# Criss-cross attention: the attention matmuls stream 96 instead of 128 columns of the turned weights

## The chip, the cores and the metric

The kernel runs on one core of a Trainium2 chip. The metric is the device time of one execution in microseconds (us). The core has TensorE (PE in the profile, with its weight loads as PEld), VectorE (DVE), ScalarE (ACT), GpSimd (POOL), SyncE (SP, which here issues all DMAs) and 16 DMA engines. SBUF is the working memory; TensorE writes into eight PSUM banks of 128 partitions x 512 fp32 values.

## The reference, cut to what matters

The input x is 8 x 512 x 96 x 96 (batch, channels, rows, columns), fp32. Every position attends to the positions of its own column and its own row:

```python
q = einsum('oc,bchw->bohw', Wq, x) + bq        # 64 channels
k = einsum('oc,bchw->bohw', Wk, x) + bk        # 64 channels
v = einsum('oc,bchw->bohw', Wv, x) + bv        # 512 channels
energy_H = einsum('bchw,bcgw->bhwg', q, k) - 1e30 * eye(96)[None, :, None, :]
energy_W = einsum('bchw,bchv->bhwv', q, k)
att = softmax(concatenate([energy_H, energy_W], -1), -1)
att_H, att_W = att[..., :96], att[..., 96:]
out_H = einsum('bcgw,bhwg->bchw', v, att_H)
out_W = einsum('bchv,bhwv->bchw', v, att_W)
return gamma * (out_H + out_W) + x
```

The change is about the last two products. For one column w (or one row h) each is a matrix product of 512 channels x 96 positions with 96 positions x 96 positions.

## The kernel before, in words

Each of the 8 batches passes through the same stages, and X (all of x for one batch, 128 partitions x 4 channel tiles x 9216 positions) stays in SBUF.

1. **Projection.** 24 chunks of 384 positions. ScalarE and GpSimd split x into two fp32r parts; TensorE makes k and q (`project_kq`, L724) and v (`project_v`, L708), and the energies along rows (`row_energies`, L734). v, k, q and the exponentials go to DRAM.
2. **Column energies.** 24 groups of four columns: TensorE multiplies k and q (L745), VectorE takes maxima and sums, ScalarE the exponentials, GpSimd masks the diagonal.
3. **Attention.** 24 chunks of four columns (the column half), then 24 chunks of four rows (the row half). For a chunk, SP loads the exponentials Pe (L220) and the values V (L224). GpSimd scales Pe by the softmax factors (L388), TensorE turns it with four transposes (`turn`, L755), ScalarE copies the result from PSUM to Pt (L474), and TensorE multiplies V with it (`attend`, L766): per column or row one product for each of four channel tiles of 128. VectorE adds the four products of one column or row, 384 values per partition, to X (`add_attention`, L608). In the row half the finished parts of X are stored, and the next batch's x comes in. The batch that is last stores through its whole row half; the others store little there and do the rest in the next projection.

V, Pe, Pt and the turned PSUM tiles have three buffers, so chunk g+1 is turned before chunk g is multiplied, and SP asks for V of a chunk when the multiplication three chunks before it has ended. The PSUM output of `attend` rotates over four banks, one per column or row of the chunk. The order on each engine is the order of the program; nothing is planned at run time.

The reference's 96 positions are the contraction rows: V and Pt hold zeros in partitions 96 to 127, so a 128-row product can be used (`attend` names `V[:, ...]` and `Pt[:, ...]` over all partitions). Along the free axis the moving operand is `Pt[:, c, r * N:r * N + WIDE]` with WIDE = 128: the 96 columns of this row and 32 more, which are those of the next row or, after the last row of a chunk, 32 zeros that GpSimd writes at L413. Their results are never read: VectorE takes `[:, :, 0:N]` of each group of 128. An fp32 matmul appears in the trace as two LDWEIGHTS and two MATMULs, so the 6144 products of L766 are 12288 of each; a transpose is one of each.

Of the kernel before, what the change touches and what calls it, by code (L numbers as in the profile page):

```python
# [12 lines left out]
N = 96  # L13
POS = N * N
ROWS = 4
CP = ROWS * N
# [9 lines left out]
RING = 3  # L26
TRIPLES = CHUNKS // RING
HALVES = 2
WIDE = 128


def criss_cross_attention(nc, x, wqk_t, wv_t, bqk, bv, gamma, out):
    B, C = x.shape[0], x.shape[1]
    CT = C // P
# [15 lines left out]
    with ctx:  # L50
        def sb(name, shape, dt=F32, at=None):
            return (at or ctx).enter_context(nc.sbuf_tensor(name, shape, dt))

        def sem(name):
            return ctx.enter_context(nc.semaphore(name))
# [29 lines left out]
        with ExitStack() as s3:  # L85
            V = sb("V", [P, RING, ROWS, C], F32, s3)
            ident = sb("ident", [N, N], F32, s3)
            Pe = sb("Pe", [N, RING, ROWS, N], F32, s3)
            Pt = sb("Pt", [P, RING, CP + WIDE - N], F32, s3)
            st = sb("st", [N, 4, N], F32, s3)  # L90
# [7 lines left out]
        t_ps, f_ps, o_ps = bank[2:5], bank[5], bank[6:8] + bank[0:2]  # L98
# [47 lines left out]
        pt_padded = sem("pt_padded")  # L146
# [8 lines left out]
        def g_no(b, along, p, c):  # L155

            return b * (2 * CHUNKS) + CHUNKS * along + p * RING + c
# [10 lines left out]
        def past(s, n):  # L168

            return n + START[s]  # L170
# [195 lines left out]
        @block.gpsimd  # L366
        def _(pool):
            def split_x(b, p, c):

                for h, cts in enumerate(halves):  # L370
                    pool.wait_ge(x_hi_made, (b * CHUNKS + p * 2 + c) * HALVES + h + 1)
                    nc.gpsimd.tensor_tensor(x_split[:, c % 2, 1, cts, :], X[:, cts, bass.ds((p * 2 + c) * CP, CP)],  # L372
                                            x_split[:, c % 2, 0, cts, :].bitcast(F32), ALU.subtract)\
                        .then_inc(x_lo_made, 1)

            def mask(b, p, c):

                pool.wait_ge(c_exped, b * GROUPS + p * RING + c + 1)
                pool.sem_inc(pool_passed, 1)
                nc.gpsimd.affine_select(out=E_cols[:, c, :, :], in_=E_cols[:, c, :, :], compare_op=ALU.not_equal,  # L380
                                        fill=0.0, base=0, pattern=[[0, GROUP], [-1, N]], channel_multiplier=1)\
                    .then_inc(c_masked, 1)

            def scale(b, along, p, c):
                pool.wait_ge(p_in[c], 16 * (b * (2 * TRIPLES) + along * TRIPLES + p + 1))

                f = mx[:, along, bass.ds((p * RING + c) * ROWS, ROWS)].unsqueeze(2).to_broadcast((N, ROWS, N))
                nc.gpsimd.tensor_tensor(Pe[:, c, :, :], Pe[:, c, :, :], f, ALU.mult)\  # L388
                    .then_inc(p_scaled, 1)

            def make_ident(times_before):
                nc.gpsimd.memset(ident[:, :], 0.0).then_inc(ident_made, 1)
                pool.wait_ge(ident_made, times_before * 2 + 1)
                pool.sem_inc(pool_passed, 1)
                nc.gpsimd.affine_select(out=ident[:, :], in_=ident[:, :], compare_op=ALU.not_equal, fill=1.0,
                                        base=0, pattern=[[-1, N]], channel_multiplier=1).then_inc(ident_made, 1)

            make_ident(0)
            with pool.Fori(0, B) as b:
                with pool.Fori(0, PAIRS) as p:  # L400
                    for c in range(2):
                        split_x(b, p, c)
                with pool.Fori(0, TRIPLES - 1) as p:
                    for c in range(RING):
                        mask(b, p, c)
                mask(b, TRIPLES - 1, 0)

                pool.wait_ge(c_summed, past(c_summed, (b + 1) * (2 * GROUPS)))
                pool.sem_inc(pool_passed, 1)
                make_ident(b + 1)  # L410
                mask(b, TRIPLES - 1, 1)
                mask(b, TRIPLES - 1, 2)
                nc.gpsimd.memset(Pt[0:N, :, CP:], 0.0).then_inc(pt_padded, 1)  # L413
                nc.gpsimd.memset(Pt[N:P, :, :], 0.0).then_inc(pt_padded, 1)
                nc.gpsimd.memset(V[N:P, 0, :, :], 0.0).then_inc(v_padded[0], 1)
                for along in range(2):

                    pool.wait_ge(f_made, b * 2 + along + 1)
                    pool.sem_inc(pool_passed, 1)
                    with pool.Fori(0, TRIPLES) as p:  # L420
                        for c in range(RING):
                            scale(b, along, p, c)
# [111 lines left out]
        def _(dve):  # L534
# [64 lines left out]
            def add_attention(b, along, p, c):  # L599
                for r in range(ROWS):  # L600
                    n = g_no(b, along, p, c) * ROWS + r
                    dve.wait_ge(o_summed, past(o_summed, n + 1))
                    at = (p * RING + c) * ROWS + r
                    if along:
                        xs = X[:, :, bass.ds(at * N, N)]
                    else:
                        xs = X[:, :, :].rearrange("p t (h w) -> p t h w", w=N)[:, :, :, at]
                    nc.vector.tensor_tensor(xs, o_ps[r][:, :].rearrange("p (t n) -> p t n", t=CT)[:, :, 0:N], xs,  # L608
                                            ALU.add).then_inc(o_added, 1)

            with dve.Fori(0, B) as b:
# [81 lines left out]
        def _(pe):  # L693
# [64 lines left out]
            def attend(b, along, p, c):  # L758
# [3 lines left out]
                for r in range(ROWS):  # L762

                    pe.wait_ge(o_added, past(o_added, g * ROWS + r - 3))
                    for ct in range(CT):
                        last = nc.tensor.matmul(o_ps[r][:, ct * WIDE:(ct + 1) * WIDE],  # L766
                                                V[:, c, r, ct * P:(ct + 1) * P], Pt[:, c, r * N:r * N + WIDE],
                                                start=True, stop=True)
                    last.then_inc(o_summed, 1)

            with pe.Fori(0, B) as b:
                def step(p, c, first=False):
                    project_kq(b, p, c)
                    if first:
                        pe.wait_ge(w_lo_made, 2)

                        pe.wait_ge(o_added, past(o_added, b * (2 * CHUNKS * ROWS)))
                    project_v(b, p, c, 0)
                    project_v(b, p, c, 1)
                    row_energies(b, p, 2 * c)  # L780
                    project_v(b, p, c, 2)
                    row_energies(b, p, 2 * c + 1)

                for c in range(2):
                    step(0, c, first=(c == 0))
                with pe.Fori(1, PAIRS) as p:
                    for c in range(2):
                        step(p, c)


                pe.wait_ge(ident_made, (b + 1) * 2)
                pe.wait_ge(z_summed, b * (SUBS + GROUPS) + SUBS)
                nc.tensor.transpose(t_ps[0][0:N, 0:N], mx[:, 1, :], ident[:, :])
                nc.tensor.transpose(t_ps[0][0:N, N:2 * N], zs[:, 1, :], ident[:, :]).then_inc(st_turned, 1)

                pe.wait_ge(e_shifted, past(e_shifted, (b + 1) * SUBS))
                for c in range(RING):
                    column_energies(b, 0, c)
                with pe.Fori(1, TRIPLES) as p:
                    for c in range(RING):  # L800
                        column_energies(b, p, c)


                pe.wait_ge(ident_made, (b + 2) * 2)
                pe.wait_ge(f_turned, b * 2 + 1)
                nc.tensor.transpose(f_ps[0:N, 0:N], st[:, 0, :], ident[:, :]).then_inc(f_turned, 1)

                pe.wait_ge(pt_padded, (b + 1) * 2)  # L810
                for j in range(RING):
                    pe.wait_ge(v_padded[j], b + 1)
                turn(b, 0, 0, 0)
                for along in range(2):
                    with pe.Fori(0, TRIPLES - 1) as p:
                        for c in range(RING):
                            turn(b, along, p + (c + 1) // RING, (c + 1) % RING)
                            attend(b, along, p, c)
                    for c in range(RING):
                        if c < RING - 1:  # L820
                            turn(b, along, TRIPLES - 1, c + 1)
                        elif along == 0:
                            turn(b, 1, 0, 0)
                        attend(b, along, TRIPLES - 1, c)
# [23 lines left out]
```

## Time and profile before

| | |
|---|---|
| time, three runs | 4355.52, 4362.07 (median), 4365.45 us |
| span of the profiled execution, first to last instruction | 4357.4 us |
| PE busy | 4063.6 us, 93% |
| PEld busy | 3654.3 us, 84% |
| DVE / ACT / POOL busy | 50% / 30% / 26% |
| mean granted TensorE clock | 0.936 of full speed |
| HBM traffic | 947.78 MB, 217 GB/s over the span |

The profile gives the span of its execution and no time beside it; the span lies within the three runs' times, 4.7 us below their median. The busy share of PE counts a matmul until its result has drained, so it is not the share of the time in which the array takes in columns; for that one reads the distance between the starts of successive instructions. The granted clock is given per stretch: 1.00 is the level of 2.4 GHz, 0.50 that of 1.2 GHz. A batch takes about 540 us: some 270 us of projection, 60 us of column energies with what lies around them, and 200 us of attention.

### The profile page before, as it was taken

What the parts mean: (1) busy time and instruction counts of PE and PEld (TensorE: products, weight loads), DVE (VectorE), ACT (ScalarE), POOL (GpSimd) and SP (SyncE); (2) the same over time, 40 slices, a digit from 0 to 9 for tenths busy, and PEclk for the clock granted to TensorE, in tenths of its full rate; (3) what the DMA queues carried; (4) which work ended last, traced back from release to release, by engine and by line L of the source; (5) the groups of instructions that cost most, each with busy time, mean ns of one, the idle gap of its engine ahead of it and who ended that gap; (6) DMA issues with size and microseconds to landing.
All of it is one profiled execution on the core that took longest, in us unless ns stands there. A gap on an engine that the chain in (4) does not pass through costs nothing.

```text
span 4357.4 us, 92393 instructions
## 1 busy us (share of the span) xinstructions
PE 4063.6 (93%) x26136; PEld 3654.3 (84%) x26136; DVE 2184.9 (50%) x3932; ACT 1288.8 (30%) x2522; POOL 1148.6 (26%) x1006
## 2 busy tenths in 40 slices
PE   8989999898998999989999899997999979999897
PEld 7878988788887998879988699886988869988697
DVE  3348533485334853348433484335843358433584
ACT  3342133421334213341133411335113351133510
POOL 3322133221332213322233222332223322233211
PEclk9988999889998999979999799997999979999799
DMA  5548977489774897749977499774997749977499
GB/s 177 172 150 213 247 231 244 153 219 253 232 238 146 222 256 229 247 136 229 249 236 239 136 232 245 246 238 134 234 239 243 240 137 232 252 237 232 148 243 315
DMA packets 555124, 947.78 MB, mean 218 GB/s; under 512 B 45120, under 2 KB 383552, under 8 KB 533568
## 3 DMA queue, kind: packets, MB, share of 16 engines
q1 hardware_dynamic: 555072, 947.30, 75.2%
q14 instruction: 46, 0.38, 0.0%
q8 instruction: 6, 0.10, 0.0%
HBM read 550.77 MB, written 396.36 MB: 217 GB/s over the span
## 4 chain that ended last, share of the span: by engine, by line
PE 82%; DMA 9%; issue 3%; ACT 2%; SPq 1%; POOL 1%; DVE 0%; ACTq 0%; POOLq 0%; DVEq 0%
PE bank L708 36%; PE bank L766 26%; PE bank L724 9%; DMA Pe<-e_scratch 7%; PE bank L745 5%; PE bank L734 3%; PE bank L755 3%; ACT kq L461 1%; DMA KQ<-kq_scratch 1%; POOL Pe L388 1%; ACT E L466 1%; DMA kq_scratch<-kq 1%; POOL x_split L372 0%; SPq L224 0%; DVE X L608 0%
## 5 line engine op out<-in xcount | busy, mean ns | idle before, releaser
L708 PE MATMUL bank<-Wv_hi,x_split 128*128 128x512 f32 x4608 | 1525.6, 399 | 0.0
L766 PE MATMUL bank<-Pt,V 128*128 128x128 f32 x12288 | 1478.4, 280 | 0.0
L766 PEld LDWEIGHTS bank<-Pt,V 128*128 128x128 f32 x12288 | 1436.7, 196 | 0.0
L608 DVE TENSOR_TENSOR X<-bank,X 128x384 f32 (+1 forms) x1536 | 1115.4, 734 | 559.1 <-PE bank L766 559.0
L372 POOL TENSOR_TENSOR x_split<-X,x_split 128x768 fp32r<-128x768 f32 x384 | 702.3, 1854 | 1411.1 <-ACT x_split L435 1411.0
L555 DVE TENSOR_TENSOR v_out<-bank,bv_row 128x512 f32<-128x512 f32 x576 | 398.3, 691 | 1287.3 <-PE bank L708 1281.2
L708 PEld LDWEIGHTS bank<-Wv_hi,x_split 128*128 128x128 f32 x4608 | 867.9, 188 | 189.0 <-issue 0.5
L708 PE MATMUL bank<-Wv_lo,x_split 128*128 128x512 f32 x2304 | 912.5, 396 | 0.0
L388 POOL TENSOR_TENSOR Pe<-Pe,mx 96x384 f32<-96x384 f32 x384 | 316.6, 824 | 1288.6 <-DMA Pe<-e_scratch 1287.8
L474 ACT ACTIVATE Pt<-bank 96x384 f32<-96x384 f32 x384 | 187.3, 488 | 1424.9 <-PE bank L755 1424.9
L446 ACT ACTIVATE kq<-bank,bqk_sb 64x192 f32<-64x192 f32 x768 | 320.6, 417 | 812.1 <-PE bank L734 645.8
L708 PEld LDWEIGHTS bank<-Wv_lo,x_split 128*128 128x128 f32 x2304 | 434.3, 188 | 88.1
L745 PE MATMUL bank<-KQ,kq 128*96 (+1 forms) x1536 | 329.2, 370 | 106.4 <-ACT kq L461 91.9
L724 PE MATMUL bank<-x_split,Wqk_hi 128*128 128x384 f32 x1536 | 409.7, 348 | 16.0 <-POOL x_split L372 16.0
L745 PEld LDWEIGHTS bank<-KQ,kq 128*96 128x96 f32 x1536 | 266.4, 253 | 169.1 <-issue 164.5
L452 ACT ACTIVATE E<-E 96x192 f32<-96x192 f32 x384 | 139.7, 364 | 605.2 <-DVE E L568 585.1
L435 ACT ACTIVATE x_split<-X 128x768 fp32r (+1 forms) x384 | 303.7, 838 | 47.5 <-PE bank L766 39.1
L755 PE MATMUL bank<-ident,Pe 96*96 96x96 f32 x1536 | 201.6, 255 | 100.7 <-POOL Pe L388 100.1
L724 PEld LDWEIGHTS bank<-x_split,Wqk_hi 128*128 128x128 f32 x1536 | 266.9, 190 | 18.5 <-issue 12.1
L724 PE MATMUL bank<-x_split,Wqk_lo 128*128 128x384 f32 x768 | 259.4, 338 | 0.0
L755 PEld LDWEIGHTS bank<-ident,Pe 96*96 96x96 f32 x1536 | 152.2, 130 | 119.8 <-POOL Pe L388 106.3
L461 ACT ACTIVATE kq<-KQ 64x192 f32 (+1 forms) x384 | 202.7, 530 | 139.8 <-DMA KQ<-kq_scratch 89.2
(45 smaller groups left out, 1551.9 us busy)
## 6 DMA issues: line engine op xcount, KB each, us to landing
V<-v_scratch SPq DMA_DIRECT2D x384, 768.0 KB, 5.7
X<-in_x SPq DMA_DIRECT2D x192, 768.0 KB, 5.1
v_scratch<-v_out SPq DMA_DIRECT2D x576, 256.0 KB, 3.8
out<-X SPq DMA_DIRECT2D x192, 768.0 KB, 6.3
Pe<-e_scratch SPq DMA_DIRECT2D x384, 144.0 KB, 5.3
kq_scratch<-kq SPq DMA_DIRECT2D x384, 96.0 KB, 2.3
e_scratch<-E SPq DMA_DIRECT2D x384, 72.0 KB, 1.7
e_scratch<-E SPq DMA_DIRECT2D x192, 144.0 KB, 1.9
```

Source lines behind the costliest of these rows:

```text
L372: nc.gpsimd.tensor_tensor(x_split[:, c % 2, 1, cts, :], X[:, cts, bass.ds((p * 2 + c) * CP, CP)], x_split[:, c % 2, 0, cts, :].bitcast(F32 ...
L388: nc.gpsimd.tensor_tensor(Pe[:, c, :, :], Pe[:, c, :, :], f, ALU.mult)\
L435: nc.scalar.activation(x_split[:, j, 0, cts, :], X[:, cts, bass.ds((p * 2 + c) * CP, CP)], ACT.Copy).then_inc(x_hi_made, 1)
L446: last = nc.scalar.activation(kq[0:CQ, i, :], kq_ps[c % 2][rows, v * SP_:(v + 1) * SP_], ACT.Identity, bias=bqk_sb[rows, :])
L461: nc.scalar.activation(kq[0:CQ, v, :].rearrange("p (w h) -> p w h", w=2), src, ACT.Copy)\
L555: nc.vector.tensor_tensor(v_out[:, s, :], v_ps[t % 2][:, :], bv_row[:, :], ALU.add)\
L608: nc.vector.tensor_tensor(xs, o_ps[r][:, :].rearrange("p (t n) -> p t n", t=CT)[:, :, 0:N], xs, ALU.add).then_inc(o_added, 1)
L708: last = nc.tensor.matmul(v_ps[t % 2][:, :], x_split[:, j, lo, ct, at], w[:, ct, :], start=(ct == 0 and n == 0), stop=(ct == CT - 1 and n ...
L724: last = nc.tensor.matmul(kq_ps[j][:, 0:CP], w[:, ct, :], x_split[:, j, lo, ct, :], start=(ct == 0 and n == 0), stop=(ct == CT - 1 and n = ...
L745: last = nc.tensor.matmul(ce_ps[c][0:N, at:at + N], kq[:, v, r * N:(r + 1) * N], k, start=True, stop=True)
L755: last = nc.tensor.transpose(t_ps[c][0:N, r * N:(r + 1) * N], Pe[:, c, r, :], ident[:, :])
L766: last = nc.tensor.matmul(o_ps[r][:, ct * WIDE:(ct + 1) * WIDE], V[:, c, r, ct * P:(ct + 1) * P], Pt[:, c, r * N:r * N + WIDE], start=True ...
```

## The change

WIDE becomes 96. Each matmul of L766 then streams the 96 columns of its own row, its four outputs lie next to each other in the first 384 columns of the bank, Pt shrinks from 416 to 384 columns per buffer, and the memset of its last 32 columns goes, with one step of the semaphore `pt_padded`. The zero partitions 96 to 127 stay. No instruction moves to another place in any engine's order; GpSimd has one memset less per batch and a narrower one (L414: 1152 columns for 1248).

```diff
-WIDE = 128
+WIDE = 96
@@ GpSimd, before the attention stage of each batch
-                nc.gpsimd.memset(Pt[0:N, :, CP:], 0.0).then_inc(pt_padded, 1)
                 nc.gpsimd.memset(Pt[N:P, :, :], 0.0).then_inc(pt_padded, 1)
@@ add_attention
-                    nc.vector.tensor_tensor(xs, o_ps[r][:, :].rearrange("p (t n) -> p t n", t=CT)[:, :, 0:N], xs,
+                    nc.vector.tensor_tensor(xs, o_ps[r][:, 0:CT * WIDE].rearrange("p (t n) -> p t n", t=CT)[:, :, 0:N], xs,
                                             ALU.add).then_inc(o_added, 1)
@@ TensorE, before the first turn of each batch
-                pe.wait_ge(pt_padded, (b + 1) * 2)
+                pe.wait_ge(pt_padded, b + 1)
```

The matmul itself reads WIDE and is written as before:

```python
last = nc.tensor.matmul(o_ps[r][:, ct * WIDE:(ct + 1) * WIDE],
                        V[:, c, r, ct * P:(ct + 1) * P], Pt[:, c, r * N:r * N + WIDE],
                        start=True, stop=True)
```

## Rows read from the trace of the kernel before

**Rows 1.** Page, part 4: the chain that ended last, by engine and line.
```profile
PE 82%; DMA 9%; issue 3%; ACT 2%; SPq 1%; POOL 1%; DVE 0%; ACTq 0%; POOLq 0%; DVEq 0%
PE bank L708 36%; PE bank L766 26%; PE bank L724 9%; DMA Pe<-e_scratch 7%; PE bank L745 5%; PE bank L734 3%; PE bank L755 3%; ACT kq L461 1%; DMA KQ<-kq_scratch 1%; POOL Pe L388 1%; ACT E L466 1%; DMA kq_scratch<-kq 1%; POOL x_split L372 0%; SPq L224 0%; DVE X L608 0%
```

**Rows 2.** Page, part 5: busy us, mean ns of one, idle before.
```profile
L766 PE MATMUL bank<-Pt,V 128*128 128x128 f32 x12288 | 1478.4, 280 | 0.0
L766 PEld LDWEIGHTS bank<-Pt,V 128*128 128x128 f32 x12288 | 1436.7, 196 | 0.0
```

**Rows 3.** Busy time by stretch; last three columns clock, DMA share, GB/s.
```profile
305.00:338.00 33.00, 31.30 (x145) 25.34 (x145) 26.93 (x55) 28.38 (x54) 9.47 (x18) 0.50 0.28 80
350.00:355.00 5.00, 5.00 (x26) 5.00 (x25) 1.65 (x2) 0.49 (x1) 0.82 (x1) 0.50 0.97 252
356.00:440.00 84.00, 84.00 (x772) 84.00 (x772) 76.55 (x86) 10.56 (x22) 17.32 (x21) 1.00 0.93 233
446.00:500.00 54.00, 53.67 (x486) 52.88 (x486) 31.15 (x55) 6.45 (x14) 11.52 (x14) 1.00 1.00 235
500.00:549.00 49.00, 40.95 (x341) 39.84 (x340) 20.63 (x38) 4.75 (x10) 7.41 (x9) 0.94 1.04 274
4250.00:4340.00 90.00, 69.69 (x607) 66.47 (x607) 37.91 (x68) 8.02 (x17) 13.99 (x17) 1.00 1.06 326
```

**Rows 4.** Chain of waits inside the column half: start us, us, piece.
```profile
928.89 0.33 PE bank L755 x4
929.23 3.60 PE bank L766 x32
932.83 0.33 PE bank L755 x4
```

**Rows 5.** Single weight loads in order of time, full clock: start us, us.
```profile
356.39 0.13 PEld L755 LDWEIGHTS bank<-ident,Pe 96*96 96x96 f32 x1
356.50 0.13 PEld L755 LDWEIGHTS bank<-ident,Pe 96*96 96x96 f32 x1
...
356.75 0.19 PEld L766 LDWEIGHTS bank<-Pt,V 128*128 128x128 f32 x1
356.86 0.19 PEld L766 LDWEIGHTS bank<-Pt,V 128*128 128x128 f32 x1
356.97 0.19 PEld L766 LDWEIGHTS bank<-Pt,V 128*128 128x128 f32 x1
```

**Rows 6.** The same at half clock, first loads of an attention stage.
```profile
350.25 0.34 PEld L766 LDWEIGHTS bank<-Pt,V 128*128 128x128 f32 x1
350.47 0.33 PEld L766 LDWEIGHTS bank<-Pt,V 128*128 128x128 f32 x1
350.68 0.33 PEld L766 LDWEIGHTS bank<-Pt,V 128*128 128x128 f32 x1
```

**Rows 7.** Chain of waits, projection stage: the row energies.
```profile
1103.56 0.34 PE bank L734 x4
```

**Rows 8.** TensorE in order of time: a stage start, and a fall of the clock.
```profile
350.41 6.25 PE L766 MATMUL bank<-Pt,V 128*128 128x128 f32 x32
...
4237.42 3.76 PE L766 MATMUL bank<-Pt,V 128*128 128x128 f32 x32
4243.66 0.88 PE L755 MATMUL bank<-ident,Pe 96*96 96x96 f32 x4 [2.48 <-POOL Pe L388]
4244.33 4.95 PE L766 MATMUL bank<-Pt,V 128*128 128x128 f32 x32
```

**Rows 9.** VectorE in order of time, column half.
```profile
902.79 3.57 DVE L608 TENSOR_TENSOR X<-bank,X 128x384 f32 x4 [0.37 <-PE bank L766]
```

**Rows 10.** Instructions on tile Pt: ns min/median/max, first and last start.
```profile
L413 POOL MEMSET Pt<- x8: 176/180/181, 343.5 to 4126.3; 96x96 f32 x8
```

**Rows 11.** Chain of waits at the start of an attention stage.
```profile
885.38 5.41 DMA Pe<-e_scratch
```

## The prediction

> **What bounds the kernel now.** I read the page's chain first: TensorE is 82% of it, L766 alone 26% and L755 3%, and the loads of Pe are 7% [rows 1]. So the changed matmuls lie on the path, with some 26% of 4357.4, about 1130 us. The second view is the busy time by stretch, because the attention stage is not one thing. In the column half TensorE never pauses (84.00 of 84.00 us) and the DMA engines are at 0.93. In the row half TensorE still hardly pauses, but the DMA share is 1.00; at its end, and through the row half of the batch that is last, it is 1.04 to 1.06 and TensorE waits [rows 3]. Third, the chain inside the column half: 0.33 us for four transposes and 3.60 us for 32 matmuls, nothing else, so a chunk takes 3.93 us [rows 4]. A pair of weight load and matmul therefore takes 3.60 / 32 = 112.5 ns. The question is which of the two sets it. The totals do not tell: both are busy for nearly the same time [rows 2]. Last I read single loads one after another, and the granted clock.
>
> **Is it the load or the streaming?** For the streaming: the row energies, 96 columns moving against 96-column weights, take 0.34 / 4 = 85 ns each [rows 7], and the L766 pairs with 128 against 128 take 112.5. Both numbers fit two passes of the moving columns at 2.4 GHz (80 and 107 ns) plus about 5, and both fit a load of the same width. The case that separates them is a wide load behind a narrow matmul, which occurs once per chunk. The first 128-column load of L766 starts at 356.75, while the last 96-column transposes are still streaming (a transpose takes 0.33 / 4 = 83 ns [rows 4]). If streaming set the pace, the next load would start 0.08 us later. It starts 0.11 later, at 356.86, and the one after it again 0.11 later [rows 5]. At half clock the same place shows 350.25 to 350.47, 0.22 us, then 0.21 [rows 6]; a 96-column matmul takes about 0.16 there. So loading 128 columns of V takes as long as streaming the 128 padded columns twice, at either clock level, and the load is not touched by the change. The matmul becomes shorter than the load that hides behind it, and the pair stays where it is.
>
> By the Trainium skill ("TensorE: Matmul & The Clock Gate", "LDWEIGHTS") a load takes its columns divided by 1.2 GHz, 107 ns for 128. The 0.11 us agree at full clock. The same page ("What happens when you issue a matmul", step FILL) says throughput is purely N cycles, which by itself would let the pair fall with the moving columns; the same rows disagree.
>
> **The change part by part**, against the profiled execution, whose span is 4357.4 us.
>
> 1. *The pair.* The new pair is set by the load. Two successive loads behind the transposes take 356.75 to 356.97, 0.22 us for two with 0.01 of rounding, so 105 to 115 ns each; not above 112.5, since that is the pair that waits for both. I take 111, between the 110 read and the present 112.5, since load and matmul hand over to each other in either case: 1.5 ns x 32 pairs x 192 column chunks = 9 us saved; ends 0 and 7.5 ns x 6144 = 46 us. In the row half I count nothing, since DMA is at 1.00 there [rows 3].
> 2. *The first transpose of a chunk.* Its load now waits for a 128-column matmul: 356.39 to 356.50, 0.11 us [rows 5]. Behind a 96-column matmul it should take 0.085: 0.025 x 192 = 5 us saved, ends 0 and 10 (both halves).
> 3. *The start of each attention stage.* The clock stands at 0.50 through the column energies, where TensorE streams 96-column matmuls with pauses (145 in 33 us), and still at 350 to 355 [rows 3]. It came back inside the first chunk: 32 starts took about 6.1 us [rows 8], and with 0.213 us for a pair at half and 0.112 at full clock this is 25 pairs at half. Before, these pairs kept the array streaming without a gap. Now each pair is a load of 0.217 and a stream of 0.16, so the array pauses in every pair, as it does in the column energies, where the clock did not come back. Only at the next four transposes does it stream without a gap again. I expect the clock to return later, after 16 more pairs: 16 x (0.217 - 0.110) = 1.7 us, times 8 = 14 us lost. Ends: 0, and what rival 4 says.
> 4. *The end of the row half.* A wait of 2.48 us for Pe is followed by transposes of 0.88 us and 32 matmuls of 4.95, against 3.76 for the same 32 before it: the clock had fallen, and that cost 1.2 us in the matmuls and about 0.4 in the transposes [rows 8]. The stretch 500 to 549 has clock 0.94 for the same reason [rows 3]. Waits of this kind stay, because they come from DMA, while the array streams a quarter less between them. I expect two more such falls per batch: 2 x 1.6 x 8 = 25 us. DMA is at 1.04 there, and while TensorE is slow the transfers go on, so I take half, 13 us; ends 0 and 50 (twice as many, none hidden).
> 5. *VectorE.* L608 is 3.57 us per column chunk with 0.37 us of waiting [rows 9]. Reading four neighbouring groups of 96 instead of four of 128 changes neither its elements nor, by that row, what it holds up. Nothing; if the pair fell, VectorE would be next, at 3.57.
> 6. *GpSimd.* One memset of 180 ns goes from each batch [rows 10] and the other shrinks by a thirteenth. TensorE waits there for the first load of Pe, 5.41 us [rows 11], which hides both. Nothing; without that cover 8 x 0.18 = 1.4 us saved.
>
> Sum: -9 - 5 + 14 + 13 = +13 us, a span of 4370. The span lies 4.7 us below the median of the runs, so I forecast 4362 + 13 = 4375 us.
>
> On padding the Trainium skill speaks against the change too: the same page ("HAM oscillation") advises, for thin matmuls, to regroup them or to pad, because the clock goes down when the array idles. In this trace it stood at 0.50 in the column energies; that it does so because of 96 columns behind 128-column loads, no row shows yet.
>
> **The rivals.**
>
> 1. *The clock behaves as before* (not slower). For it: the row half of the last batch keeps 1.00 with TensorE busy only 69.69 of 90 us [rows 3], so full clock is not lost easily. Against: the 0.50 all through 305 to 338 [rows 3]. Then only terms 1 and 2 are left: -14, 4348 us. It decides if the first chunk of a stage again gets its clock back within some 25 pairs.
> 2. *Streaming set the pace after all.* The pair falls to 85 ns and a chunk to 32 x 0.085 + 0.33 = 3.05 us; but DMA at 0.93 allows 3.93 x 0.93 = 3.65, just above VectorE's 3.57. 0.28 x 192 = 54 us saved, nothing in the row half: 4308 us. Against it stand rows 5 and 6; for it only the fit of 85 and 112.5.
> 3. *The change does nothing to the time.* The pair stays at 112.5 with the load, the matmul's end is off the path, and the clock's losses are about 0 or are paid back by terms 1 and 2: 4362 us.
> 4. *The clock stays down for long* (much slower). At half clock a column chunk takes 32 x 0.217 + 0.66 = 7.6 us, 3.7 more than now. If six chunks of each batch more run so, 48 x 3.7 = 176 us: 4538 us. For it: nothing in the new stream is free of pauses but the transposes. Against: at full clock the stretch 4250 to 4340, with its waits, kept 1.00.
>
> **How the numbers follow.** Chances: forecast 0.42 (own range 4366 to 4400), rival 1 0.21, rival 2 0.05, rival 3 0.21, rival 4 0.11. A difference of 0.2%, 9 us, is about what can be told from no change. Faster: rival 2, and three quarters of rival 1, 0.21. Same: rival 3, the rest of rival 1 and 0.06 of the forecast, 0.32. Slower: the rest of the forecast and rival 4, 0.47. The range 4343 to 4430 takes in terms 3 and 4 at their upper ends and rival 1; outside lie rival 2 and most of rival 4, with tails of the others.
>
> **What would show it.** The L766 loads of the changed kernel start 0.11 us apart at full clock and 0.22 at half, with a single matmul some 30 ns shorter: step "load or streaming" is right. Starts 0.085 apart would make it wrong. A column chunk should go from 3.93 to 3.86. At the start of each attention stage the granted clock should return during the second chunk, not the first, and at the end of the row half more chunks should show 32 matmuls of 5 us or more. If the clock's mean stays at 0.936, terms 3 and 4 were wrong; if it falls below 0.88, rival 4 was right. The forecast is wrong if the time is below 4353.

## The result and the profile after

The changed kernel is slower by a little: 4365.02 us median of 18 runs (4359.04 to 4373.81) against 4358.98 of 18 (4348.89 to 4369.62); the ratio is 1.0018, with a 95% interval of 1.0009 to 1.0026, so 4 to 11 us, 8 at the ratio. The profiled execution took 4368.17 us, with a span of 4366.3.

The page of the changed kernel (busy us and share; the chain by line; then busy us, mean ns of one, idle before). Lines past L413 are one lower than before: L765 is the old L766, L754 the old L755, L607 the old L608.

```profile
PE 4078.1 (93%) x26136; PEld 3671.2 (84%) x26136; DVE 2196.7 (50%) x3932; ACT 1288.0 (29%) x2522; POOL 1144.5 (26%) x998
...
PE bank L707 36%; PE bank L765 26%; PE bank L723 9%; DMA Pe<-e_scratch 7%; PE bank L744 5%; PE bank L733 3%; PE bank L754 3%; ACT kq L460 1%; DMA KQ<-kq_scratch 1%; POOL Pe L388 1%; DMA kq_scratch<-kq 1%; ACT E L465 1%; POOL x_split L372 0%; DVE st L668 0%; SPq L224 0%
...
L765 PE MATMUL bank<-Pt,V 128*128 128x96 f32 x12288 | 1496.6, 282 | 1.9 <-ACT Pt L473 1.7
L765 PEld LDWEIGHTS bank<-Pt,V 128*128 128x128 f32 x12288 | 1463.7, 199 | 4.4 <-issue 4.4
L607 DVE TENSOR_TENSOR X<-bank,X 128x384 f32 (+1 forms) x1536 | 1115.2, 733 | 556.5 <-PE bank L765 556.3
```

TensorE and its loads are busier by 15 and 17 us (4063.6 and 3654.3 us before), with the same number of instructions, although each attention matmul streams a quarter less. The chain has the same shape as before [rows 1].

Busy time by stretch, columns as in [rows 3] (PE, PEld, DVE, ACT, POOL, then granted clock, DMA share, GB/s):

```profile
351.00:354.00 3.00, 3.00 (x17) 3.00 (x15) 0.89 (x1) 0.00 (x0) 0.82 (x1) 0.50 0.99 230
357.00:440.00 83.00, 83.00 (x768) 83.00 (x766) 75.76 (x86) 10.30 (x22) 16.93 (x21) 1.00 0.95 237
446.00:500.00 54.00, 53.02 (x480) 52.36 (x481) 30.00 (x54) 6.80 (x14) 10.95 (x14) 1.00 1.01 231
500.00:549.00 49.00, 43.57 (x338) 43.02 (x337) 20.71 (x38) 4.38 (x9) 7.40 (x9) 0.86 1.00 257
4250.00:4340.00 90.00, 74.35 (x582) 72.37 (x581) 36.00 (x65) 7.78 (x16) 13.15 (x16) 0.90 1.04 311
```

At a stage's start, in the column half and in the first part of the row half the clock is what it was. In 500 to 549 it went from 0.94 to 0.86, and in the row half of the last batch from 1.00 to 0.90, with TensorE busy 74.35 of 90 us instead of 69.69 [rows 3]. DMA moves less in both (257 and 311 GB/s for 274 and 326).

The chain inside the column half, against [rows 4]:

```profile
929.80 0.33 PE bank L754 x4
930.14 3.57 PE bank L765 x32
933.71 0.33 PE bank L754 x4
```

The matmuls' 3.57 us for 3.60 hold the whole difference, with rounding: over the distances between full-clock column chunks of the trace the median went from 3.932 to 3.906 us, 26 ns. Single weight loads show where it went (start us, us; the kernel before, then the changed one):

```profile
928.51 0.19 PEld L766 LDWEIGHTS bank<-Pt,V 128*128 128x128 f32 x1
928.62 0.13 PEld L755 LDWEIGHTS bank<-ident,Pe 96*96 96x96 f32 x1
...
929.45 0.19 PEld L765 LDWEIGHTS bank<-Pt,V 128*128 128x128 f32 x1
929.53 0.15 PEld L754 LDWEIGHTS bank<-ident,Pe 96*96 96x96 f32 x1
...
929.89 0.19 PEld L765 LDWEIGHTS bank<-Pt,V 128*128 128x128 f32 x1
930.00 0.19 PEld L765 LDWEIGHTS bank<-Pt,V 128*128 128x128 f32 x1
```

The load of a chunk's first transpose starts 84 ns after the load before it and not 111 (medians of the column chunks); the loads of V stay 0.11 us apart (112 ns, median of both kernels).

TensorE in order of time (start us, us, instruction, count, wait): a stage start, and two falls of the clock at the end of a row half, against [rows 8]:

```profile
350.48 5.65 PE L765 MATMUL bank<-Pt,V 128*128 128x96 f32 x32 [0.28 <-ACT Pt L473]
355.96 0.49 PE L754 MATMUL bank<-ident,Pe 96*96 96x96 f32 x4
356.29 3.74 PE L765 MATMUL bank<-Pt,V 128*128 128x96 f32 x32
...
518.09 0.81 PE L754 MATMUL bank<-ident,Pe 96*96 96x96 f32 x4 [1.45 <-POOL Pe L388]
518.69 6.76 PE L765 MATMUL bank<-Pt,V 128*128 128x96 f32 x32
...
535.52 0.88 PE L754 MATMUL bank<-ident,Pe 96*96 96x96 f32 x4 [2.26 <-POOL Pe L388]
536.18 6.56 PE L765 MATMUL bank<-Pt,V 128*128 128x96 f32 x32
```

The same places of the kernel before (the chunk behind the wait at 518, and the next one that fell):

```profile
518.95 0.53 PE L755 MATMUL bank<-ident,Pe 96*96 96x96 f32 x4 [1.32 <-POOL Pe L388]
519.32 3.76 PE L766 MATMUL bank<-Pt,V 128*128 128x128 f32 x32
...
530.00 5.25 PE L766 MATMUL bank<-Pt,V 128*128 128x128 f32 x32
```

The first chunk takes 5.65 us (6.25 before), so the clock returns inside it, as it does in all eight batches of both traces. But 32 matmuls at the end of the row half now take 6.56 and 6.76 us against 3.74: nearly the whole chunk runs at half clock. At 518 nearly the same wait (1.45 us, 1.32 before) is followed by half clock now and was not before. In the last twelve row chunks of all batches the clock fell 10 times before and 18 times after, and of the fallen chunks 1 of 10 took over 6 us from the first start to the last before, 9 of 18 after. From the clock's record: in the last twelve row chunks of the eight batches 37 us were spent at half clock before, 92 after, and by the starts of their matmuls these chunks together took 467.9 us before and 474.9 after, 7 us more.

### The profile page after: what moved, and what is told of

Its sections match the earlier page's. It is cut to its first block, busy times and chain, and to the rows that moved or that the text cites. A ratio compares the mean times of both kernels' runs of the same rounds, so it can differ in the third digit from the quotient of the medians.

```text
span 4366.3 us, 92385 instructions
## 1 busy us (share of the span) xinstructions
PE 4078.1 (93%) x26136; PEld 3671.2 (84%) x26136; DVE 2196.7 (50%) x3932; ACT 1288.0 (29%) x2522; POOL 1144.5 (26%) x998
## 4 chain that ended last, share of the span: by engine, by line
PE 81%; DMA 9%; issue 3%; ACT 2%; DVE 1%; POOL 1%; SPq 1%; ACTq 0%; POOLq 0%; DVEq 0%
PE bank L707 36%; PE bank L765 26%; PE bank L723 9%; DMA Pe<-e_scratch 7%; PE bank L744 5%; PE bank L733 3%; PE bank L754 3%; ACT kq L460 1%; DMA KQ<-kq_scratch 1%; POOL Pe L388 1%; DMA kq_scratch<-kq 1%; ACT E L465 1%; POOL x_split L372 0%; DVE st L668 0%; SPq L224 0%
## 5 line engine op out<-in xcount | busy, mean ns | idle before, releaser
L765 PE MATMUL bank<-Pt,V 128*128 128x96 f32 x12288 | 1496.6, 282 | 1.9 <-ACT Pt L473 1.7
L765 PEld LDWEIGHTS bank<-Pt,V 128*128 128x128 f32 x12288 | 1463.7, 199 | 4.4 <-issue 4.4
L607 DVE TENSOR_TENSOR X<-bank,X 128x384 f32 (+1 forms) x1536 | 1115.2, 733 | 556.5 <-PE bank L765 556.3
L754 PE MATMUL bank<-ident,Pe 96*96 96x96 f32 x1536 | 200.8, 255 | 79.0 <-POOL Pe L388 78.4
L754 PEld LDWEIGHTS bank<-ident,Pe 96*96 96x96 f32 x1536 | 152.9, 135 | 92.3 <-POOL Pe L388 79.8
```

The source lines that it names most:

```text
L607: nc.vector.tensor_tensor(xs, o_ps[r][:, 0:CT * WIDE].rearrange("p (t n) -> p t n", t=CT)[:, :, 0:N], xs, ALU.add).then_inc(o_added, 1)
L754: last = nc.tensor.transpose(t_ps[c][0:N, r * N:(r + 1) * N], Pe[:, c, r, :], ident[:, :])
```

## The experiments

Each ratio is against the kernel before, run beside it. The theory: the load of 128 columns of V sets the pair, so nothing is gained by streaming less; the loss comes from the clock, which falls more often, or for longer, between the waits of the row half. The rivals: the new place of the outputs or another cost in every chunk; nothing but scatter.

**Which half loses.** Two kernels (e1, e2) choose the width by half; the outputs are placed, and VectorE reads them, by the same width. Cut:

```diff
+WIDES = (96, 128)      # e2: (128, 96)
-    Pt[:, c, r * N:r * N + WIDE]
+    Pt[:, c, r * N:r * N + WIDES[along]]
```

> 96 columns in the column half only, 128 as before in the row half. Clock theory (the loss of the change, 0.18% or 8 us, comes from the clock falling more often between the waits of the row half, while the column half gains a few us by its transposes): 4355 to 4359 us for 4359 before, a ratio of 0.999 to 1.000, and no more falls of the clock in the row half than before. Rival (the packed outputs or something else in every chunk costs the 8 us): half of it here, ratio 1.001. Rival (nothing but scatter): 1.000.

Measured (e1): 4353.87 us against 4358.9, ratio 0.9985 (0.9975 to 0.9995). In its trace the last twelve row chunks took 464.7 us in sum, with 48 us and 13 falls at half clock, near the kernel before (467.9, 37 and 10). This is the fastest kernel that computes everything, by 0.15% against the kernel before and by 0.33% against the changed one.

> 128 columns in the column half, 96 in the row half only. Clock theory: the whole loss and a little more, since the gain of the column half is gone: ratio 1.002 to 1.003, and the sum over the batches of the last twelve row chunks some 7 us longer than before. Rival (a cost in every chunk): ratio 1.001. Rival (scatter): 1.000.

Measured (e2): 4370.79 us, ratio 1.0020 (1.0010 to 1.0031). In the trace the column chunks are at 3.932 us again; the last twelve row chunks took 492.7 us in sum, of which 120 at half clock. That is 25 us longer than before where I had expected 7, but the traced execution was the slowest of the twelve. So the two halves go opposite ways: 96 columns gain 0.15% in the column half and lose 0.2% (e2) to 0.33% (the changed kernel against e1) in the row half. The rival with a cost in every chunk is out.

**The place of the outputs.** 128 columns stream, but outputs start 96 apart, and VectorE reads them there (e3). Cut:

```diff
-    nc.tensor.matmul(o_ps[r][:, ct * WIDE:(ct + 1) * WIDE],
+    nc.tensor.matmul(o_ps[r][:, ct * N:ct * N + WIDE],
```

> 128 columns stream as before, but each output starts 96 columns after the one before, so that the next matmul overwrites the padding and VectorE reads 384 neighbouring columns as in the changed kernel. Clock and load theory: the time of before, ratio 0.999 to 1.001, VectorE's adds unchanged at 0.73 us. Rival (the new place of the outputs costs the 8 us): ratio 1.002.

Measured (e3): 4359.2 us, ratio 1.0002 (0.9994 to 1.0011); one add of VectorE takes 734 ns as before. The layout costs nothing that can be told, and by the interval at most 5 us.

**Load or streaming.** Loads of 96 of each 128 columns of V, with 96 columns streamed (e5, from the changed kernel) and with 128 (e6, from the kernel before); output and addition shrink to 96 partitions, so the attention of a quarter of the channels is left out. Cut:

```diff
-    V[:, c, r, ct * P:(ct + 1) * P]
+    V[:, c, r, ct * P:ct * P + 96]
```

> The changed kernel with weight loads of 96 of each 128 columns of V, so a quarter of the channels gets no attention. Load theory: the pair of load and matmul falls from 0.112 to 0.085 us, the column chunk from 3.93 us to what comes next, the transfers (0.93 x 3.93 = 3.65 us) or VectorE (3.57): about 3.65, 0.28 x 192 = 54 us less, ratio 0.986 to 0.990; the row half stays. Rival (something else holds the pair at 0.112, such as the issue of instructions): 0.112 and the time of the changed kernel, ratio 1.002.

Measured (e5): 4325.82 us, ratio 0.9917 (0.9902 to 0.9931). The chain in the column half (start us, us, piece):

```profile
928.99 5.80 DMA Pe<-e_scratch
...
934.96 0.84 POOL Pe L388
...
935.84 0.54 PE bank L754 x4
936.38 2.79 PE bank L765 x32
```

32 pairs in 2.79 us, 87 ns (85 between most starts). The load had set the pair. The chunk does not fall with it: TensorE waits for Pe, whose transfer of 5.80 us is in the chain, DMA stands at 1.03 in 900 to 980, and the chunks of this half, from the second on, come 3.79 us apart on average, not 3.65. The next bound, the transfers, was named rightly; the gain it leaves, 37 us in all, was taken too high at 54.

> The kernel before with weight loads of 96 columns only and 128 streamed, a quarter of the channels without attention. Load theory: the streaming now sets the pair alone, 0.112 us as before, ratio 1.000. Rival (the load sets the pair and streaming has slack even at 128): 0.085 to 0.1, ratio 0.99.

Measured (e6): 4337.81 us, ratio 0.9943 (0.9928 to 0.9957), which the theory as I had put it did not give. The chain in the column half:

```profile
930.56 0.33 PE bank L755 x4
930.89 3.50 PE bank L766 x32
```

32 pairs in 3.50 us are 109.4 ns. So with a 96-column load in front, streaming 128 columns takes 109; with a 128-column load the pair takes 112 whether 128, 112 (e8) or 96 columns stream. The kernel before was already bound by the load, by about 3 ns. This is why narrower streaming gave nothing per pair. The column chunk is 3.83 us here, 0.10 less, which over 192 chunks is 20 of the 25 us.

Two widths above and between, outputs 96 apart (`WIDE = 144` in e7, `WIDE = 112` in e8, both with the outputs of e3):

> 144 columns streamed, outputs 96 apart. Load theory: past 128 the streaming is the longer of the two, 288 / 2.4 + 5 = 125 ns a pair, a column chunk of 4.33 us, 0.4 x 192 = 77 us more in the column half and some 0.4 x 12 x 8 = 38 in the first half of the row half, together about 115 us, ratio 1.022 to 1.030; fewer falls of the clock than before. Rival (the load sets the pair with room to spare): 0.112, ratio 1.000.

Measured (e7): 4459.8 us, ratio 1.0228 (1.0213 to 1.0243). The chain:

```profile
943.95 0.33 PE bank L755 x4
944.28 3.95 PE bank L766 x32
```

3.95 / 32 = 123 ns: here streaming is the longer. Only 14 us at half clock are left in the last twelve row chunks of all batches.

> 112 columns streamed, outputs 96 apart. Load theory: pairs of 0.112 us at full clock, as with 96 and 128, a first transpose of 0.098; falls of the clock in the row half between those of 128 and 96: ratio 1.000 to 1.001. Rival (streaming sets part of the pace): faster than before, 0.995.

Measured (e8): 4363.14 us against 4362.7, ratio 1.0002 (0.9993 to 1.0011). Starts are 112 ns apart, the load of the first transpose starts 98 ns after the load before it, column chunks take 3.919 us, and 44 us are at half clock in the last twelve row chunks. Both effects lie between those of 96 and 128.

**How far from the edge.** 64 (e4) and 88 (e9) columns streamed and added, in the changed kernel; a third and a twelfth of the attention is left out. Cut, of e9:

```diff
-    nc.tensor.matmul(o_ps[r][:, ct * WIDE:(ct + 1) * WIDE], ..., Pt[:, c, r * N:r * N + WIDE],
+    nc.tensor.matmul(o_ps[r][:, ct * 88:(ct + 1) * 88], ..., Pt[:, c, r * N:r * N + 88],
```

> Only 64 of the 96 columns are streamed and added, so a third of the attention is left out; the weight loads are the same. Load theory: pairs of L765 still 0.112 us apart at full clock, column chunks still 3.93 us less 0.02 or so, and the clock falls more often still, so the time is no shorter: ratio 1.00 to 1.03. If the clock does not return at the start of the attention stages, up to 1.2. Rival (streaming sets the pace at least in part): pairs of 0.06 to 0.1 us and column chunks down to what the transfers allow, 3.65 us, ratio 0.987.

Measured (e4): 5568.62 us, ratio 1.2776 (1.2758 to 1.2795), beyond even the 1.2 that I had allowed. In the trace the granted clock is 0.50 in 345 to 700, and a column chunk takes 0.64 + 6.77 = 7.41 us. So the clock does not return, and the pairs at full clock that the expectation spoke of never came; e4 and e9 say nothing of them.

> 88 of the 96 columns streamed and added, so a twelfth of the attention is left out. The pair at full clock stays 0.112 us apart. Theory that the clock's return needs only a somewhat denser stream than that of 64 columns, for which it never returned: it returns in the first or second chunk as with 96, ratio 1.002 to 1.01. Rival (96 is already at the edge, since the array then pauses a quarter of each pair): it does not return, chunks of 7.4 us, ratio about 1.28.

Measured (e9): 5584.09 us in two runs, ratio 1.281 (1.2788 to 1.2832), what the rival said and not the theory. Busy time by stretch of the kernel with 88 columns, columns as before, and its chain:

```profile
345.00:700.00 355.00, 351.16 (x1695) 350.58 (x1696) 129.11 (x192) 24.77 (x49) 40.23 (x49) 0.50 0.57 143
```

```profile
402.57 0.64 PE bank L754 x4
403.21 6.81 PE bank L765 x32
```

The granted clock is 0.50 through every attention stage, and a chunk takes 0.64 + 6.81 = 7.45 us. With 96 columns the clock comes back inside the first chunk, with 88 never: the changed kernel stands within 8 columns of a loss of 28%.

**Where in the row half; and the start.** The next three kernels (e10, e11, e12) split TensorE's row-half loop, so that the last twelve row chunks of a batch have a width of their own. Cut:

```diff
+LATE, REST = 128, 96      # e11: 96, 128
-    with pe.Fori(0, TRIPLES - 1) as p:
+    for lo, hi, wide in (((0, 4, REST), (4, TRIPLES - 1, LATE)) if along else ((0, TRIPLES - 1, REST),)):
+        with pe.Fori(lo, hi) as p:
```

> 96 columns in the column half and the first twelve row chunks, 128 in the last twelve, where TensorE waits for transfers; outputs 96 apart throughout. Clock theory: the falls that cost time are in those last twelve; ratio 0.998 to 0.999, as with 96 in the column half alone. Rival (the falls come in the whole row half): 1.000 to 1.001.

Measured (e10): 4383.63 us, ratio 1.0056 (1.0043 to 1.0069).

> The opposite: 128 columns everywhere but in the last twelve row chunks of each batch, which stream 96. Clock theory: the whole loss of the row half, without the gain of the column half: ratio 1.002 to 1.003, some 50 us more at half clock in those chunks. Rival: about 1.001, half of it.

Measured (e11): 4396.62 us, ratio 1.0088 (1.0074 to 1.0103). The last twelve row chunks have 75 us at half clock in its trace, 37 more than the kernel before and not 50; e10 has 58.

Both expectations failed, because the split has a cost of its own. The page's instruction queue of the first one, and TensorE where the second batch begins (columns as above):

```profile
q8 instruction: 70, 1.15, 0.1%
...
548.70 5.38 PE L767 MATMUL bank<-Pt,V 128*128 128x128 f32 x44
556.17 0.98 PE L725 MATMUL bank<-x_split,Wqk_hi 128*128 128x384 f32 x2 [2.09 <-ACT x_split L436]
```

The instruction queue q8 moved 0.10 MB in 6 packets in the kernels without the split, and 1.15 MB in 70 here. When TensorE goes back to the top of the batch loop it stands still before L725: from the start of the last attention matmul to the first of L725 it is 1.9 to 2.4 us in each of seven batches, a distance of under 0.1 us before. The row names ScalarE's x_split as what ended the wait, but its first piece had ended at 552.3, and in the trace TensorE's queue issues nothing at all from 553.8 to 555.8. The trace shows a transfer of q8 there: in all 21 standstills of e10, e11 and e12 one packet of 16 KB is on its way when the queue stops (at 552.97 to 554.28 here), and the queue goes on 1.4 to 1.6 us after that packet has ended. So the queue very probably waits for its own instructions; no run changes this alone.

The standstills are some 15 us in all, and the split cost about 30, if e10 is compared with e1 and e11 with e2 by ratio. By chunk, e10 loses the other half, 17 us, to e1 in three chunks of each batch: the last column chunk and the fourth and fifteenth row chunks are longer by 0.34, 0.65 and 1.1 us. The two kernels share this cost, so they are compared with each other: 96 columns in the last twelve row chunks alone are 13 us slower than 96 everywhere but there. That agrees in sign and roughly in size with e2 against e1 (17 us), but it does not say alone that the first twelve row chunks are harmless.

The last kernel (e12) is e10 with 20 matmuls per batch whose results are not read, in TensorE's waits before the attention. Cut:

```diff
+            def warm(n):
+                for _ in range(n):
+                    nc.tensor.matmul(v_ps[0][:, :], Wqk_hi[:, 0, :], Wv_hi[:, 0, :], start=True, stop=True)
+                warm(12)
                 pe.wait_ge(ident_made, (b + 2) * 2)
...
+                warm(4)
                 pe.wait_ge(pt_padded, (b + 1) * 2)
...
                 turn(b, 0, 0, 0)
+                warm(4)
```

> As 96 columns with 128 in the last twelve row chunks, and besides 20 matmuls per batch of 512 columns whose results are never read, put where TensorE waits between the column energies and the first attention matmul (12 before the factors are turned, 4 before and 4 after the first turn). If the clock is granted by what the array does before, it is at 1.00 when the attention starts, and the first 25 or so pairs of each stage take 0.112 us instead of 0.217: 2.6 us x 8 = 20 us less, ratio 0.994 to 0.996. If the first chunks wait for their transfers anyway, or the clock falls again before, 0.998 to 0.999. If the added matmuls delay the turns, above 0.999.

Measured (e12): 4361.48 us, ratio 1.0007 (0.9998 to 1.0016) against before; against e10, to which these matmuls are the only addition, 22 us less. TensorE in order of time:

```profile
340.63 3.77 PE L774 MATMUL bank<-Wv_hi,Wqk_hi 128*128 128x512 f32 x12
...
346.94 1.17 PE L774 MATMUL bank<-Wv_hi,Wqk_hi 128*128 128x512 f32 x4
348.62 0.51 PE L756 MATMUL bank<-ident,Pe 96*96 96x96 f32 x4 [0.51 <-POOL Pe L389]
348.91 1.84 PE L774 MATMUL bank<-Wv_hi,Wqk_hi 128*128 128x512 f32 x4
350.55 0.84 PE L756 MATMUL bank<-ident,Pe 96*96 96x96 f32 x4
351.19 4.40 PE L767 MATMUL bank<-Pt,V 128*128 128x96 f32 x32
```

The first 32 attention matmuls take 4.40 us, with the first seven still at half clock, instead of 5.65 in the changed kernel; in the other batches they start within 3.5 to 3.7 us. The time at half clock in the column halves goes from 45 us in e10 to 2. So the expectation's mechanism holds: the clock at the start of a stage is set by what TensorE did before. Its ratio does not hold, because of the split, and the 22 us are not all the clock's. By chunk, the first one of a stage is 2.2 us shorter than in e10 and the second 0.2 longer, 16 us in all. The rest goes with chunks that the split had made longer and that are as in e1 again (the last column chunk, the fourth and the fifteenth row chunk), while two others grew; what moved them is not traced. These matmuls in e1, without the split, were not run.

## Why the prediction was right, and in what wrong

It forecast 13 us of loss; the ratio says 8 (4 to 11). In time, 4375 us were forecast and 4365 measured, 1 us below the forecast's own range of 4366 to 4400. Of these 10 us, 3 are the base: a run's time lies 1.8 to 1.9 us above its span in every run that has both, so the span of 4357.4 belongs to 4359 and not to 4362, and 4359 is what 18 runs gave. The loss of 0.18% is also just under the 0.2% that I had called about the least that can be told; 18 runs of each kernel tell it from none. Step by step:

1. *The pair* (9 us saved): the mechanism right, the size wrong, 0. Starts are 112 ns apart before and after. I had read a gain from rounding, 0.22 us for two loads, and from a pair of 112.5 ns that held the turn to the transposes. e6 shows the reason: the load, at 112, was already longer than the streaming, at 109. What the step stood on, that the load does not let the pair fall to 85, is shown by e5. One sign did not come: a single matmul is not 30 ns shorter but lasts 275 ns in both traces, which decides nothing, since the ends of matmuls are modelled.
2. *The turn to the transposes* (5 us saved): right in size, one place off. 26 ns per column chunk, times 192, is 5 us; e1 shows it as 0.15% with an interval of 0.05 to 0.25%. But the two loads that I read, 356.39 and 356.50, are those of the first and second transpose, and they are 0.11 us apart in the changed kernel too. What shrank is the distance before them, from the last load of V to the first transpose's: 111 ns with 128 columns streamed, 98 with 112, 84 with 96. The column chunk went to 3.906 us, not to the 3.86 that terms 1 and 2 gave together.
3. *The start of the stages* (14 us lost): wrong, 0. The clock returns inside the first chunk as before, after 18 to 24 of its 32 pairs (11 to 25 before); the column halves have 37 us at half clock, and had 35. What I feared, a clock that does not come back behind a narrower stream, happens at 88 columns and at 64, and not at 96. That the pause in every pair is the cause fits this but is not shown by itself.
4. *The end of the row half* (13 us lost): right, in size too. e1 against the changed kernel differs in the row half's width alone, and by ratio it is 0.33%, 14 us (11 by the medians). In detail it was otherwise: I had expected two more falls per batch, half hidden. The traces show one more per batch (10 falls before, 18 after), but longer ones: those of 518 and 536 last about a whole chunk. Together they come to 55 us more at half clock, which at 213 ns a pair for 112 would cost 26 us if nothing hid it, the 25 of the forecast; the chunks took 7 us longer than before and 10 longer than in e1. That half would be hidden rested on no number, so the nearness of the 13 is in part luck.
5. *VectorE and GpSimd* (terms 5 and 6, nothing): right, as far as e3 shows it for the layout; the memset was not tried by itself.

The two wrong terms, -9 and +14, almost cancelled. That is luck, and it makes the sum look better than its parts; what is left, -5 + 13 = +8, is what was measured.

Rival 1 (the clock as before) fails by e1 against the changed kernel and by the time at half clock, 92 us for 37. Rival 2 (streaming sets the pace) fails by the starts, and e5 shows that even a pair of 85 ns would have given 37 us, not 54. Rival 3 (nothing changes) lies outside the ratio's interval here and describes e8. Rival 4 did not come, but e9 shows that it was nearer than its 0.11 let a reader think.

## What to carry to other kernels

Where every matmul has its own weight load, compare the two before narrowing the moving operand: behind a load of 128 columns, streaming 96 or 112 fp32 columns instead of 128 saved nothing per pair here, and padding up to 128 cost only 26 ns at each turn from the attention matmuls to the transposes. Padding may even earn its place by keeping the clock up where TensorE has to wait for transfers; so choose the width by stage, as e1 does, and look at the granted clock of each stage, not at its mean (0.936 and 0.932 here). Test one step beyond a width that works: between 96 and 88 columns the loss went from 0.2% to 28%.

## What the runs showed of the hardware that I had not expected

- The stream of 88 columns behind 128-column loads never got its clock back (0.50 for every attention stage, chunks of 7.45 us), while that of 96 did within one chunk, in every batch of the changed kernel.
- A pair of load and matmul took 112 ns with 128 columns loaded and 96, 112 or 128 streamed, 109 with 96 loaded and 128 streamed, 123 with 144 streamed, and 85 to 87 with 96 and 96.
- Splitting one loop of TensorE cost about 30 us per execution (e10 against e1, e11 against e2, by ratio): instruction transfers of 1.15 MB instead of 0.10, and some 2.2 us of standstill at each return to the top of the batch loop (15 us in all), which ended 1.4 to 1.6 us after a packet of q8 had landed, 21 times of 21.
- Matmuls that do no work, in a wait before a stage, took 43 us of half clock out of the column halves, worth 16 us of the 22 by which e12 is faster than e10.
